# The next chunk's preparation starts three steps earlier and runs over 31 steps; ACT's copies of the middle and low part of B come later

## The reference

```python
xc, z = split(x @ W_in.T)
xs = silu(conv3(xc))                       # three taps along the sequence
dt_param, Bp, Cp = split(xs @ W_x.T)       # 64, 16, 16
dt = softplus(dt_param @ W_dt.T + b_dt) + 1e-5
A = exp(-exp(A_log) * dt[..., None])       # 256 x 16 per token
Bx = Bp[:, :, None, :] * dt[..., None] * xs[..., None]
s = A * s + Bx                             # along the sequence
y = (Cp @ W_C.T) * s.sum(-1) + D_param * xs
out = (y @ W_out.T) * silu(z)
```

## Time and profile before

| | us |
|---|---|
| median of three runs | 1206.76 (1205.27 to 1210.16) |
| the profiled execution | 1218.7 |
| its span in the trace | 1216.9 |
| PE busy | 1025.6 (84%) |
| DVE busy | 670.7 (55%) |
| ACT busy | 645.0 (53%) |
| POOL busy | 688.0 (57%) |
| first scan to last scan | 40.0 to 660.3 |

### The profile page before, as it was taken

The page is one execution under the profiler, slowest core; times in us unless marked ns, Lnnn a source line. Parts: engine busy times, 40 slices in busy tenths (PEclk is TensorE's granted clock), DMA queues, the critical chain, the costliest instruction groups (busy, mean ns, idle before and its releaser), DMA issues.

```text
span 1216.9 us, 15544 instructions
## 1 busy us (share of the span) xinstructions
PE 1025.6 (84%) x4704; PEld 830.0 (68%) x4704; DVE 670.7 (55%) x1153; ACT 645.0 (53%) x1247; POOL 688.0 (57%) x668
## 2 busy tenths in 40 slices
PE   5436597878977878958979897999999999999996
PEld 3204265656755556747757785889999999998885
DVE  5999997998998989866985241011100010000333
ACT  4776769787496785686672431233333333333342
POOL 0696958686499895788796356443343333322211
PEclk9667588888787988989989898999999999999999
DMA  9110100202002034141574475899999988873511
GB/s 299 45 35 1 65 5 20 68 17 70 1 18 70 1 101 160 45 108 32 148 190 144 138 205 126 231 253 269 310 307 323 295 255 255 265 228 77 171 65 52
DMA packets 143571, 166.40 MB, mean 137 GB/s; under 512 B 26712, under 2 KB 128624, under 8 KB 143472
## 3 DMA queue, kind: packets, MB, share of 16 engines
q1 hardware_dynamic: 127616, 146.43, 37.0%
q0 software_dynamic: 15872, 18.99, 8.4%
HBM read 138.94 MB, written 26.87 MB: 136 GB/s over the span
## 4 chain that ended last, share of the span: by engine, by line
PE 56%; DVE 12%; issue 11%; POOL 10%; ACT 7%; SPq 1%; DMA 1%; DVEq 0%; POOLq 0%; ACTq 0%
PE psum L1092 24%; PE psum L1059 12%; PE psum L1048 7%; PE psum L1071 6%; DVE S L1277 5%; POOL Ssum L1678 5%; DVE psum L1252 2%; ACT A L1548 2%; PE psum L933 1%; PE psum L1035 1%; PE psum L1014 1%; PE psum L994 1%; POOL xs L1653 1%; POOL list_d L1697 1%; ACT hT L1587 1%
## 5 line engine op out<-in xcount | busy, mean ns | idle before, releaser
L1678 POOL TENSOR_TENSOR Ssum<-Ssum,S 128x512 f32<-128x512 f32 x240 | 303.3, 1283 | 89.9 <-DVE S L1277 89.1
L1092 PE MATMUL psum<-w,hT 128*128 128x256 f32 x1152 | 262.1, 385 | 14.9 <-issue 12.3
L1092 PEld LDWEIGHTS psum<-w,hT 128*128 128x128 f32 x1152 | 220.0, 193 | 47.4 <-issue 14.7
L1728 POOL DMA_INDIRECT acc_d<-y,ID x72 | 114.3, 1587 | 240.4 <-ACT y L1598 112.7
L1548 ACT ACTIVATE A<-dts,nea 128x512 f32<-128x512 f32 x256 | 175.2, 717 | 78.3 <-DVE S L1277 62.9
L1059 PE MATMUL psum<-XT,w 128*128 128x256 f32 x800 | 189.8, 394 | 16.4 <-issue 10.1
L1252 DVE TENSOR_TENSOR psum<-us,psum 128x512 f32<-128x512 f32 x256 | 163.3, 684 | 50.7 <-PE psum L978 50.2
L1059 PEld LDWEIGHTS psum<-XT,w 128*128 128x128 f32 x800 | 156.5, 197 | 47.2 <-issue 16.6
L1277 DVE TENSOR_TENSOR_SCAN S<-A,carry,psum 128x512 f32<-128x512 f32 x120 | 148.7, 1267 | 0.0
L1048 PE MATMUL psum<-nT,s 128*128 128x256 f32 x512 | 134.8, 422 | 10.8 <-DVE nb L1290 10.3
L1598 ACT ACTIVATE y<-psum,ID 128x256 f32<-128x256 f32 x72 | 30.1, 470 | 213.9 <-DVE psum L1395 213.9
(11 more groups left out here) (160 smaller groups left out, 1226.6 us busy)
## 6 DMA issues: line engine op xcount, KB each, us to landing
w<-W SPq DMA_DIRECT2D x94, 1024.0 KB
bb<-b SPq DMA_DIRECT2D x47, 128.0 KB
xnb<-x SPq DMA_DIRECT2D x16, 256.0 KB, 3.0
Xr<-x SPq DMA_DIRECT2D x16, 256.0 KB
x_d<-gb SPq DMA_DIRECT2D x8, 512.0 KB, 2.9
xn_d<-nb SPq DMA_DIRECT2D x8, 512.0 KB
X<-x_d SPq DMA_DIRECT2D x16, 256.0 KB, 7.5
ACC<-acc_d SPq DMA_DIRECT2D x16, 256.0 KB, 5.4
```

Source lines behind the costliest of these rows:

```text
L1092: t = eng.matmul(bank(g)[:, 256 * k:256 * k + 256], hT[n % 2][:, f, 128 * k:128 * k + 128], w[:, f, :], start=f == 0, stop=f == 7)
L1678: eng.tensor_tensor(to, to, of, ALU.add).then_inc(nsum, 1)
L1728: eng.indirect_dma_start(acc_d, bass.IndirectOffsetOnAxis(ap=ID[:, col, 1:2].bitcast(u32), axis=0), y[n % NY][:, k, :], None, compute_op=A ...
```

## The change

`prep` gets 31 pieces instead of 28, and its first three pieces run in steps 29, 30 and 31 of the chunk two in front. What stood at steps 0 to 14 moves one to three steps forward, what stood at step 18 or later stays within a step or two. Inside `prep`, for chunks 1 to 7, `mid_out` goes behind both `dt_out` and `low_out` three pieces later. For chunk 1, which has nothing in front, the first four pieces come at once in step 0 of chunk 0. No instruction is added or removed; the expert work, placed by free banks, moves with it.

```diff
-FIRST_POST, LAST_POST, FIRST_PREP, LAST_PREP = 0, 27, 0, 27
+FIRST_POST, LAST_POST, FIRST_PREP, LAST_PREP = 0, 27, -3, 27
...
             yield
             yield
             yield
+            yield
         else:
...
         say("dt", i, 1, t1)
         say("dt_out", i, 0, t0)
-        say("mid_out", i)
-        yield
-        say("low", i)
+        if not i:
+            say("mid_out", i)
+        yield
+        if not i:
+            say("low", i)
         say("dt_out", i, 1, t1)
-        yield
+        if i:
+            say("mid_out", i)
+        yield
+        if i:
+            say("low", i)
         say("softplus", i, t0, t1)
+        yield
+        yield
+        yield
         say("low_out", i)
-        yield
-        yield
-        yield
         yield
...
+    ahead, done_prep = prep(1), 0
+
+    def prepare(k):
+
+        nonlocal done_prep
+        want = min(n_prep, -(-n_prep * (k + 1 - FIRST_PREP) // (LAST_PREP + 1 - FIRST_PREP)))
+        part(ahead, want - done_prep)
+        done_prep = max(want, done_prep)
+
     for i in range(NC):
...
-            if k >= FIRST_PREP:
-                want = min(n_prep, -(-n_prep * (k + 1 - FIRST_PREP) // (LAST_PREP + 1 - FIRST_PREP)))
-                part(ahead, want - done_prep)
-                done_prep = max(want, done_prep)
+            if k == LAST_PREP + 1:
+                part(ahead, 99)
+                ahead, done_prep = prep(i + 2) if i + 2 < NC else iter(()), 0
+            if k <= LAST_PREP or k >= 32 + FIRST_PREP:
+                prepare(k if k <= LAST_PREP else k - 32)
```

More of the change, by code:

```diff
@@ L182, in prep @@
         say("dt_out", i, 0, t0)
-        say("mid_out", i)
+        if not i:
+            say("mid_out", i)
         yield
-        say("low", i)
+        if not i:
+            say("low", i)
         say("dt_out", i, 1, t1)
+        if i:
+            say("mid_out", i)
         yield
+        if i:
+            say("low", i)
         say("softplus", i, t0, t1)
-        say("low_out", i)
         yield
@@ L192, in prep @@
         yield
+        say("low_out", i)
         yield
@@ L479, in timetable @@
         pass
+    ahead, done_prep = prep(1), 0
[4 more added lines that the diff above has]
+        done_prep = max(want, done_prep)
     for i in range(NC):
-        ahead = prep(i + 1) if i + 1 < NC else iter(())
         behind = post(i - 1) if i else iter(())
-        done_post = done_prep = 0
+        done_post = 0
         for k, _ in enumerate(main(i)):
@@ L499, in timetable @@
         part(behind, 99)
-        part(ahead, 99)
     last = post(NC - 1)
```

## The result

| | us |
|---|---|
| kernel before, median of 12 runs | 1207.5 (1205.3 to 1210.2) |
| changed kernel, median of 12 runs | 1215.4 (1210.7 to 1217.5) |
| ratio | 1.0062 (95%: 1.0049 to 1.0076) |

The forecast was 1198.5, with a range of 1188 to 1211. The time lies above the range, and the sign is the other one.

A forecast was written before the change was run, and what follows sets the result against it. DVE's multiplies and scans bound the first stage, PE's work the tail. Gains 3.3, 1.6, 10.6, 7.0 less losses 2.0, 3, 8.9 give 8.6 us won; from the 1206.76 median, 1198, given as 1198.5 (1188 to 1211).

The forecast's parts named there:

- a stall of 2.8 "a pair later": Chunk 6: DVE's 4.25 us stall becomes one of 2.8 us, a pair later.
- the 6.34: Chunk 6: DVE's 6.34 us wait falls to 0.9 us, since xs is ready long before `dbc`.
- the 8.53: Chunk 6: DVE's 8.53 us wait goes, since the copy of `dbc` comes ahead of the GELU pass.
- a new one of 7.6 behind nT: Chunk 6: new 7.6 us DVE stall, as nT waits for normals that stand behind the GELU pass.
- The sum for chunks 2 to 5: Chunks 2 to 5: 3.3 us won at step 17, 2.0 lost at chunk starts, 1.6 won by later copies.
- 7.0 won: Chunk 7: DVE's idle time falls from 12.4 to 5.4 us as downs waiting for the pass move behind spreads.
- 3.4: End of chunk 7: 3.4 us of DVE waiting left, from 10.3 us against three pairs of 3.4 each.
- 3 lost: Tail, last scan to end of logits: 43.5 us instead of 40.5, for one more down and a turn.
- one set of 1 MB: Tail: weights formerly fetched before the logits are fetched behind them, 5 us; counted only in a rival.
- my own signs of being wrong: Load of x late at step 29, last scan under 10 us earlier, or PE's gaps behind the logits growing.
- PE carries its work into the tail: Rival, chance 0.16: tail loses 17 us (8.9 + 3 + 5), total 1210 to 1220; with 10 won, 1214.
- the first rival: Most waits only change their name: chunks 6 and 7 win 8.6 instead of 17.6 us, total 1207; chance 0.27.

The follow-up runs named there:

- e11: The changed kernel with only the tail's GELU pass moved behind normal 3 of chunk 7, on a slow chip: 1223.1 us, ratio 1.0031.
- e10: The changed kernel run again unaltered, as the control on a slow chip: 1227.4 us, ratio 1.0067 to the kernel before.

## Why the prediction was wrong

**Right.** The reading of the first stage by its names. In chunks 2 to 5 the stall moved from the spread to the statistics, which wait for POOL's residual sum. In chunk 6 I had written a stall of 2.8 "a pair later" (3.60), the 6.34 nearly gone (it is gone), the 8.53 gone, and a new one of 7.6 behind nT (7.90). The small waits there fell further than the 4.0 I took, to 1.7 us (85.1 - 71.9 less the two long ones). One of them was the 3.97 for a turn, so that not every long wait ended with a spread, as I had said. The load of x at step 29 was never waited for. The five downs behind the logits took 8.88 us against 8.9.

**Right by luck.** The sum for chunks 2 to 5, 3.5 won against 2.9. By chunk it is 4.0 and 2.6 won in chunks 2 and 4, 0.3 and 2.8 lost in chunks 3 and 5. Step 17 of chunk 2 alone won 4.0 of its 6.4 us, not 1.4, and the longer wait for POOL's sum at the start of chunk 5 (4.47 against 1.85) stood in no term.

**The step that failed first: "7.0 won" in chunk 7.** It measured 1.1 lost. I followed the second GELU pass alone. The first one, which the table of the change shows going from step 4 to step 7, I left out, and it has just the pattern that I had named for the end of this chunk: a spread behind a down that waits for the pass. It gave 3.98, with 1.71 and 2.14 at the start of the chunk; at the end 5.56 came instead of 3.4. That 3.4 was no result of its own working either, for 10.3 against three pairs of 3.4 leaves 0.1. DVE's idle time there went from 12.5 us (80.6 - 68.1) to 15.3 (81.7 - 66.4), not to 5.4.

**The second: "3 lost" in the chain to the logits.** It measured 6.7. I counted the parts that stand in the chain and not where the GELU pass falls in it. The sentence that all 18 expert groups of the first stage come before the tail was wrong: in both kernels the pass and the downs of the last pair stand behind the last scan. Of the 6.7 us, 6.0 are PE's longer waits (2.82 + 8.40 against 4.20 + 0.98), by the rows of both traces; e11 wins 4.3 of it back by moving the pass alone.

**The third: a term I had and left out of the sum.** That one set of 1 MB is now fetched behind the logits, for 5 us, stood among the rivals. A wait came, at 4.88 us, though not for the slot that I named, but for the bias of the first fetch behind the lists, whose place in the plan fell from 11 parts ahead of its use to 8. The stretch behind the logits is 11.6 longer, 2.7 more than my term.

Together these are 8.1 + 3.7 + 2.7 = 14.5 us against the forecast, 2.9 for it in chunks 2 to 6, 0.9 against it ahead of chunk 2, where I had no term for chunk 0: 12.5, which is the step from -8.6 to the +3.9 of the traces. The medians are 4.0 further apart than the traces, which I can't assign to a stretch. Of my own signs of being wrong, one came: PE's idle time behind the logits grew, from 15.3 to 17.1 us.

**The chances.** The rival "PE carries its work into the tail" had nearly the right numbers: 17 lost in the tail (18.3), "with 10 won, 1214" (1215.4). The second number is in part luck, for with the 14.4 won of the traces that sum gives 1209. I gave it 0.16, since I believed in 17.6 won in chunks 6 and 7 (11.8). Its five parts could be counted in the order, and the gain it was set against was a sum of five estimates. In the first rival the 9 us taken off don't follow from what is named: 1.45, 5.4 and 3.5 make 10.4.

**The clock.** The sum took every part at 1.78 us and was warned of waits. In chunk 6 the granted clock rose from 0.92 to 0.98 with fewer waits, and it fell from 0.96 to 0.86 in the last chain, where PE waits longer; 24 rows of down behind the 8.40 us took 6.76 us against 5.35. The two parts behind nT cost 1.7 us more (5.30 against 3.57), not the 3 I had warned of. The rule that I had quoted of the Trainium skill (TensorE: Matmul & The Clock Gate, What's actually happening: the throttled clock is the default, and activity releases it) agrees with the rows of chunk 6 and of the chain. The Trainium skill, Perfetto Trace Analysis, Identifying the Most-Contended Engine, takes weight loads and not matmul busy time as a measure of TensorE's headroom. The weight loads do show room in chunk 7 (53.8 us of 81.7), but it was not to be had, since the queue's head waited for ACT (3.98 us at 592.42).

## What to carry to other kernels

In a kernel with two stages of different limits, won time in the first counts only less what it pushes into the second: count the work behind the boundary in the order itself, before any estimate of stalls; that term came true here (8.88 against 8.9 us), while the sum of stalls in chunk 7 was off by 8.1. When a change shifts one stream of steps, follow every long instruction of the others (here each GELU pass, the first of chunk 7 and the one in the tail too), not only the one that hurts now. And a change that moves a balance should be timed with the balance set again: on quick chips the same edit was 0.6% slower with 54 advances and 0.5 to 0.65% faster with 58.

## What the runs showed of the hardware

The kernel before takes 10 to 13 us more on chips 10, 11 and 5 than on 12 and 1, and the changed one 12.0 more on chip 11 than in the table of the result. With the changed kernel the two traces are the same up to the logits (694.5 and 694.2) and differ behind them (517.3 and 530.1 us). On the slow chip (e10) PE idles in ten pieces, 10.99 us in all between 739 and 757, while POOL writes the last lists. PE and POOL in e10:

```profile
742.21 0.38 PE L1107 MATMUL psum<-w,hT 128*128 128x256 f32 x1 [1.74 <-issue]
744.30 0.58 PE L1107 MATMUL psum<-w,hT 128*128 128x256 f32 x1 [1.71 <-issue]
...
742.57 0.96 POOL L1712 DMA_INDIRECT list_d<-VAL,posi  x1 [0.30 <-issue]
743.84 0.96 POOL L1712 DMA_INDIRECT list_d<-VAL,posi  x1 [0.30 <-issue]
```

In the quick trace POOL does the same at the same pace (an instruction every 1.26 us from 735.30 on), and PE has no idle piece there. No release by another engine is shown, and neither the cause nor that it goes with the chip and not with something else of those runs is settled. It matters for reading: the first trace of the kernel before had this, and with it 10 us of its tail that its three timed runs did not have.
